# A mixture-of-experts kernel on one core: x loaded first, quaternions as rows, the bias of z written by ScalarE, five low halves subtracted by GpSimd

## What is computed

```python
# x: (8, 512, 256), so 4096 tokens of 256; 8 experts with a hidden width of 1024, the best 2 per token
def cond(x):                       # gate over the sequence, then a quaternion rotation
    x_filtered = ifft(fft(x_quat, axis=1) * spectral_gate, axis=1).real
    return hamilton(q_left_n, hamilton(x_filtered, q_right_conj))
def ffn(x):
    h = x @ W_in + b_in                                  # z in the kernel
    logits = h @ W_gate + b_gate
    topv, topi = top_k(softmax(logits), 2)
    topv = topv / sum(topv)
    mid  = relu(einsum('nd,edh->neh', h, W1) + b1)
    eout = einsum('neh,ehd->ned', mid, W2) + b2
    return (sum over the two choices of topv * eout) @ W_out + b_out
out = x + ffn(cond(x))
```

## Time and profile before

| | |
|---|---|
| median of 3 runs | 512.32 us (510.97 to 513.12) |
| profiled execution | 515.1 us, its span 513.2 us |
| TensorE busy | 494.9 us, 96% of the span |
| VectorE busy | 380.6 us, 74% |
| ScalarE busy | 283.2 us, 55% |
| GpSimd busy | 217.5 us, 42% |
| granted TensorE clock | 1.000 |
| DMA | 80.62 MB |

### The profile page before, as it was taken

The page is one execution under the profiler, slowest core; times in us unless marked ns, Lnnn a source line. Parts: engine busy times, 40 slices in busy tenths (PEclk is TensorE's granted clock), DMA queues, the critical chain, the costliest instruction groups (busy, mean ns, idle before and its releaser), DMA issues.

```text
span 513.2 us, 14538 instructions
## 1 busy us (share of the span) xinstructions
PE 494.9 (96%) x4658; PEld 430.7 (84%) x4659; DVE 380.6 (74%) x742; ACT 283.2 (55%) x576; POOL 217.5 (42%) x264
## 2 busy tenths in 40 slices
PE   7889998899999999999999999999899999999997
PEld 7556687788888888888888888889799999998786
DVE  4789987677786776878768787676568887864675
ACT  3533544655666556665566665336668778780221
POOL 4500025048456384464844637435545453321121
PEclk9999999999999999999999999999999999999999
DMA  6406534846556464555645543433354445133983
GB/s 225 158 2 209 190 125 124 237 143 205 139 172 188 140 213 131 164 179 155 198 144 163 175 122 93 115 100 99 91 163 150 135 130 150 34 114 126 406 333 140
DMA packets 75812, 80.62 MB, mean 157 GB/s; under 512 B 42983, under 2 KB 61740, under 8 KB 74732
## 3 DMA queue, kind: packets, MB, share of 16 engines
q1 hardware_dynamic: 56912, 41.44, 26.2%
q0 software_dynamic: 7936, 22.29, 13.0%
q10 hardware_dynamic: 10908, 16.17, 9.9%
HBM read 53.40 MB, written 26.48 MB: 156 GB/s over the span
## 4 chain that ended last, share of the span: by engine, by line
PE 83%; DMA 5%; issue 5%; DVE 3%; ACT 2%; ACTq 1%; SPq 0%; another core or an unknown queue 0%; DVEq 0%
PE bank L1399 24%; PE bank L1386 10%; PE bank L1325 8%; PE bank L1326 7%; PE bank L1327 7%; PE bank L1218 5%; PE bank L1455 5%; PE bank L1372 4%; PE bank L1374 4%; PE bank L1373 4%; DMA gq<-rows_by_slot 2%; DMA w1s<-y_by_choice 1%; PE bank L1465 1%; PE bank L1188 1%; DMA brow<-in_L_ffn_b_in 1%
## 5 line engine op out<-in xcount | busy, mean ns | idle before, releaser
L713 ACT ACTIVATE region<-bank,b1p,cbits 128x256 f32<-128x256 f32 (+1 forms) x368 | 163.1, 522 | 131.9 <-PE bank L1327 51.7
L567 POOL DMA_INDIRECT y_by_choice<-region,dst x71 | 87.3, 1229 | 166.9 <-DVE region L1063 151.5
L1399 PE MATMUL bank<-w2s,region 128*128 x1200 | 136.0, 273 | 0.9 <-issue 0.7
L1399 PEld LDWEIGHTS bank<-w2s,region 128*128 128x128 f16 x1200 | 116.7, 98 | 16.7 <-issue 2.9
L1094 DVE TENSOR_TENSOR region<-region 128x512 f16<-128x512 f32 (+1 forms) x184 | 104.0, 575 | 27.7 <-ACT region L697 20.4
L1325 PE MATMUL bank<-region,w1s 128*128 128x256 f16 x384 | 104.7, 273 | 4.3 <-DVE region L1100 2.2
L1327 PE MATMUL bank<-region,w1s 128*128 128x256 f16 x384 | 104.7, 273 | 0.0
L1326 PE MATMUL bank<-region,w1s 128*128 128x256 f16 x384 | 104.7, 273 | 0.0
L559 POOL DMA_INDIRECT region<-z_by_token,src x71 | 71.9, 1013 | 75.4 <-DVE src L1020 50.6
L1090 DVE CAST region<-region 128x512 f16<-128x512 f32 x100 | 46.0, 460 | 52.1 <-ACT region L713 47.9
L1372 PE MATMUL bank<-region 128*128 128x128 f16 x336 | 57.5, 219 | 1.1 <-DVE region L1100 0.5
(11 more groups left out here) (267 smaller groups left out, 644.4 us busy)
## 6 DMA issues: line engine op xcount, KB each, us to landing
region<-in_L_ffn_W ACTq DMA_DIRECT2D x14, 1024.0 KB
rows_by_slot<-region SPq DMA_DIRECT2D x33, 256.0 KB
gq<-rows_by_slot SPq DMA_DIRECT2D x132, 64.0 KB
w1s<-y_by_choice SPq DMA_DIRECT2D x12, 512.0 KB, 11.1
w1s<-in_x SPq DMA_DIRECT2D x8, 512.0 KB, 8.3
z_by_token<-w1s SPq DMA_DIRECT2D x16, 256.0 KB, 2.1
region<-in_L_ffn_W SPq DMA_DIRECT2D x2, 1024.0 KB
region<-in_x SPq DMA_DIRECT2D x8, 256.0 KB
```

Of the source, the lines that this page charges most:

```text
L567: g.indirect_dma_start(out=ybuf, out_offset=bass.IndirectOffsetOnAxis(ap=at, axis=0), in_=ysb[:, a % 2, h, :], in_offset=None).then_inc(s_ ...
L713: m = s.activation(midf[:, b, c * n:(c + 1) * n], FB[b][:, c * n:(c + 1) * n], ACT.Relu, bias=b1p[:, bass.ds(r, 1), f:f + 1].rearrange("p ...
L1399: last = mm(YB[par][:, h * D:(h + 1) * D], mids[:, par, l, b, c * TS + h * P:c * TS + (h + 1) * P], w2_at(e, w, f), start=(f == 0 and l == ...
```

## The change

- Loads. `load_channels` and `load_gate` are gone. The quaternion, condition and gate values come in as rows (`qrow`), twice each, on the sync queue, and TensorE transposes them into a bank. ScalarE's queue starts with x groups 0 and 1 and `W_in`; the sync queue loads groups 2 to 7. `b3f` becomes `binb`, b_in on all 128 partitions.
- Opening. TensorE's first dummy products go from 18 to 9, and 4, 3 and 5 dummy products are put at later places. `weff` is multiplied once, scaled, and then transposed on TensorE. x pairs use four banks (`XTB`).
- z. Five dummy products overwrite the five banks. `z_bias` on ScalarE writes the bias into a bank ahead of each pair, and the four products add to it. For the pairs 4, 6, 8, 10 and 12 (`ZPOOL`) ScalarE also copies the scaled bank in full into SBUF (`z_full`, in the buffer `gq`), and GpSimd subtracts the high half from that; VectorE does the other eleven.
- Order. x maxima 5, 6 and 7 and the scale of z come later in VectorE's list; `powers` and `expert_exponents` stand behind `src`; `norms` stands behind `rows_of_slots`.

```diff
-            load_channels(sp, 0)
-            sp.dma_start(winr[:], W_in.rearrange("(k p) n -> p k n", p=P)).then_inc(s_win, 16)
-            for g in range(NG):
-                sp.dma_start(xin[:, g * XG:(g + 1) * XG], tokens(x_h, g * XG, XG)).then_inc(s_x[g], 16)
+            for half in range(2):
+                sp.dma_start(qrow[0:4, half, :], q_right).then_inc(s_q, 16)
+                sp.dma_start(qrow[4:4 + NCOND, half, :], cond).then_inc(s_q, 16)
+            load_x(sp, 2)
+            for half in range(2):
+                sp.dma_start(qrow[4 + NCOND:5 + NCOND, half, :], gate).then_inc(s_gt, 16)
+            for g in range(3, NG):
+                load_x(sp, g)
             sp.dma_start(wout[:], W_out.rearrange("(k p) n -> p k n", p=P)).then_inc(s_late, 16)
...
-            pool.wait_ge(s_b3f, 16)
-            for q in range(3):
-                link(g.tensor_copy(b3r[:, q, :], b3f[:, q, :]))
-                if q < 2:
-                    link(g.tensor_tensor(b3f[:, q + 1, :], b3f[:, q, :], b3r[:, q, :], ALU.subtract))
-            link(g.tensor_scalar(bpc[:, 0, :], b3r[:, 0, :], ident[0:3, 0:1], None, ALU.mult))
-            for q in range(1, 3):
-                link(g.tensor_scalar(bpc[:, 1, :], b3r[:, q, :], ident[0:3, q:q + 1], None, ALU.mult))
-                link(g.tensor_tensor(bpc[:, 0, :], bpc[:, 0, :], bpc[:, 1, :], ALU.add))
-            g.tensor_copy(bin3[:, 0:D], bpc[:, 0, :])
-            g.tensor_copy(bin3[:, D:2 * D], bpc[:, 0, :]).then_inc(s_b3, 1)
...
+            for n, i in enumerate(ZPOOL):
+                pool.wait_ge(s_zc, i + 1)
+                pool.wait_ge(s_zf, n + 1)
+                g.tensor_tensor(zst[:, i, :, 1, :], zfull[:, n % 2], zst[:, i, :, 0, :], ALU.subtract
+                                ).then_inc(s_zg, 1)
             pool.wait_ge(s_idx, 1)
             pool.wait_ge(s_zst, 16 * NP)
...
-            load_channels(act, 1)
+            def copy_xt(i):
+                act.wait_ge(s_xtp, i + 1)
+                s.activation(xt_sb[:, i].rearrange("p t k c -> p (t k c)"), XTB[i % 4][:], ACT.Copy
+                             ).then_inc(s_xt, 1)
+
+            load_x(act, 0)
+            load_x(act, 1)
+            act.dma_start(winr[:], W_in.rearrange("(k p) n -> p k n", p=P)).then_inc(s_win, 16)
             act.dma_start(brow[0:E * KF, :], b1.rearrange("e (c p) -> (e c) p", p=P)).then_inc(s_brow, 16)
             act.dma_start(brow[E * KF:E * KF + KD, :], b_in.rearrange("(k p) -> k p", p=P)).then_inc(s_brow, 16)
-            for half in range(2):
-                load_gate(act, half)
+            act.wait_ge(s_id, 1)
+            s.activation(qsq[:, 14:16], ident[:, 0:2], ACT.Sqrt)
+            copy_xt(0)
             act.dma_start(wgr[:], W_gate.rearrange("(k p) n -> p k n", p=P)).then_inc(s_small, 16)
             act.dma_start(bgr[:], b_gate.rearrange("(a e) -> a e", a=1)).then_inc(s_small, 16)
-            act.dma_start(b3f[:, 0, :], b_in.partition_broadcast(3)).then_inc(s_b3f, 16)
+            copy_xt(1)
+            act.dma_start(binb[:, 0, :], b_in.partition_broadcast(P)).then_inc(s_binb, 16)
+            copy_xt(2)
             act.wait_ge(s_n2, 1)
             s.activation(nrm[:, 1, :], nrm[:, 0, :], ACT.Sqrt).then_inc(s_root, 1)
+            copy_xt(3)
             s.activation(nrm[:, 8, :], nrm[:, 0, :], ACT.Exp, scale=0.0)
...
+            def z_full(n):
+                if n >= 2:
+                    act.wait_ge(s_zg, n - 1)
+                s.activation(zfull[:, n % 2], ZB[ZPOOL[n] % NZ][:].rearrange("p (c k) -> p c k", k=KD), ACT.Copy,
+                             scale=sx[:, 0:1].bitcast(f32)).then_inc(s_zf, 1)
...
-            for i in range(NP // 2):
+            for i in range(4, 11):
                 copy_xt(i)
             copy_logits(0)
-            for i in range(NP // 2, NP):
+            for i in range(11, NP):
                 copy_xt(i)
-                if i == 10:
+                if i == 13:
                     exp(0)
-                if i == 9:
+                if i == 12:
                     act.wait_ge(s_we, 1)
                     s.activation(zj[:], weff.rearrange("p k d -> p (k d)"), ACT.Square,
                                  accum_out=bss[:, E + 1:E + 2]).then_inc(s_wsq, 1)
             copy_logits(1)
+
+            def z_bias(i):
+                if i - NZ in ZPOOL:
+                    act.wait_ge(s_zf, ZPOOL.index(i - NZ) + 1)
+                elif i >= NZ:
+                    act.wait_ge(s_zlo, ZDVE.index(i - NZ) + 1)
+                else:
+                    act.wait_ge(s_zcl, i + 1)
+                s.activation(ZB[i % NZ][:].rearrange("p (t d) -> p t d", t=2), binb[:].to_broadcast([P, 2, D]), ACT.Copy
+                             ).then_inc(s_zb, 1)
+
+            act.wait_ge(s_binb, 16)
+            for i in range(2):
+                z_bias(i)
             exp(1)
+            for i in range(2, NZ):
+                z_bias(i)
             act.wait_ge(s_sx, 1)
             act.wait_ge(s_wsq, 1)
             for i in range(NP):
                 z_out(i)
-                if i == 8:
+                if i in ZPOOL:
+                    z_full(ZPOOL.index(i))
+                if 1 <= i <= NP - NZ:
+                    z_bias(i + NZ - 1)
+                if i == 9:
                     w1_squares(0)
-                if i == 10:
+                if i == 11:
                     w2_squares(0)
...
-                if i >= NZ:
-                    pe.wait_ge(s_zlo, i - NZ + 1)
-                if i == NZ - 1:
-                    pe.wait_ge(s_sx, 1)
-                mm(ZB[i % NZ][:], ones3[:], bin3[:], start=True, stop=False, skip_group_check=True)
+                pe.wait_ge(s_zb, i + 1)
...
-            for i in range(2):
+            for i in range(3):
                 x_pair(i)
+            pe.wait_ge(s_gt, 16 * 2)
+            tr(bank[6][:, 0:1 + NQ], qrow[:].rearrange("q h c -> q (h c)"), ident[0:NQ + 1, 0:NQ + 1]
+               ).then_inc(s_gp, 1)
+            pe.wait_ge(s_brow, 16 * 2)
+            tr(bank[7][:, 0:NR], brow[:], ident[0:NR, 0:NR]).then_inc(s_btp, 1)
+            pe.wait_ge(s_const, 1)
+            spin(bank[5], 4)
             pe.wait_ge(s_rt, 1)
             pe.wait_ge(s_win, 16)
             for ki in range(KD):
                 for kj in range(KD):
-                    mm(bank[1][:, ki * D:(ki + 1) * D], rt[:, kj, ki * P:(ki + 1) * P], winr[:, kj, :],
-                       start=(kj == 0), stop=(kj == KD - 1))
-            for kd in range(KD):
-                for kj in range(KD):
-                    last = mm(bank[6][:, kd * D:(kd + 1) * D], winr[:, kj, kd * P:(kd + 1) * P], rt[:, kj, :],
+                    last = mm(bank[1][:, ki * D:(ki + 1) * D], rt[:, kj, ki * P:(ki + 1) * P], winr[:, kj, :],
                               start=(kj == 0), stop=(kj == KD - 1))
             last.then_inc(s_wep, 1)
-            for i in range(2, 5):
+            for i in range(3, 7):
                 x_pair(i)
             pe.wait_ge(s_we, 1)
+            for ki in range(KD):
+                for kd in range(KD):
+                    last = tr(bank[6][:, kd * D + ki * P:kd * D + (ki + 1) * P], weff[:, ki, kd * P:(kd + 1) * P],
+                              ident[:])
+            last.then_inc(s_wtp, 1)
+            for i in range(7, 9):
+                x_pair(i)
+            pe.wait_ge(s_wt, 1)
             pe.wait_ge(s_small, 16 * 2)
             pe.wait_ge(s_const, 1)
...
             pe.wait_ge(s_wg, 1)
+            spin(bank[5], 3)
             logits_half(0)
-            x_pair(8)
+            x_pair(11)
             logits_t(0)
-            for i in range(9, NP):
+            for i in range(12, NP):
                 x_pair(i)
+            spin(bank[5], 5)
             logits_half(1)
-            pe.wait_ge(s_xmx, NG + 1)
-            tr(bank[5][0:1, 0:P], xmax[:, NG + 1:NG + 2], ident[:]).then_inc(s_xm1, 1)
+            pe.wait_ge(s_ml, 1)
+            for i in range(NZ):
+                mm(ZB[i][:], ones16[:], iota16[:].rearrange("p c q -> p (c q)").unsqueeze(1).to_broadcast([P, 2, 2 * P]),
+                   start=True, stop=True).then_inc(s_zcl, 1)
             logits_t(1)
-            pe.wait_ge(s_b3, 1)
             z_pair(0)
-            pe.wait_ge(s_xm2, 1)
-            pe.wait_ge(s_bsq, 1)
-            pe.wait_ge(s_wsq, 1)
-            mm(bank[5][:, 256:256 + E + 2], ones[:], bss[:], start=True, stop=True)
-            mm(bank[5][:, 192:193], ones[0:1, :], xtop[:], start=True, stop=True).then_inc(s_xm3, 1)
             z_pair(1)
             pe.wait_ge(s_m, LG)
             m_et = m16[:].rearrange("p e t -> p (e t)")
             mm(TB[0][:, 0:E * NT], before[:], m_et, start=True, stop=True)
             mm(TB[0][:, E * NT:2 * E * NT], ones16[:], m_et, start=True, stop=True).then_inc(s_rank, 1)
-            for i in range(2, NP):
+            z_pair(2)
+            pe.wait_ge(s_xmx, NG + 1)
+            tr(bank[7][0:1, 0:P], xmax[:, NG + 1:NG + 2], ident[:]).then_inc(s_xm1, 1)
```

(18 more changed lines are left out.)

## The result

| | before | changed |
|---|---|---|
| median of 18 runs each | 512.2 us | 515.58 us (512.75 to 518.37) |
| profiled execution, its span | 515.1, 513.2 us | 516.36, 514.6 us |
| second choices end | 36.30 | 33.24 |
| slot map ends (T) | 72.67 | 73.28 |
| first gather starts | 72.97 | 75.08 |

The ratio is 1.0075, with a 95% interval of 1.0054 to 1.0097. On 512.2 that is 3.8 us; the medians lie 3.4 apart. The forecast was 515.0. The number was close, but its terms were not: they missed in both directions and happened to cancel. What follows is mostly about that.

What follows compares the result with a forecast made beforehand. TensorE and VectorE were taken as nearly level up to the slot map's end, which moves the rest. Terms -2.4 + 0.1 + 5.1 + 0.2 = +3.0, rounded down to +2.7 on 512.32, gave 515.0 us; range 509.2 to 517.8.

Steps and rivals of the forecast that it cites:

- Opening, -2.4: Start to second choices: row loads and four x banks end the second choices at 33.9 instead of 36.30, 2.4 us earlier.
- Rival C, late rows: Opening: rows queue behind x and land at 8.1, so it gains 0.3, not 2.4; with hold-up 517.1 us; chance 0.13.
- VectorE from there to T without hold-ups, +0.1: Second choices to slot map's end: work taken off VectorE is offset by moved-in maxima and waits; 36.5 against 36.4 us.
- The waits for banks: VectorE during z: new waits because ScalarE frees banks for their bias in order; 2.5 us with handovers.
- the opening's gain is eaten by what moved behind it: VectorE behind the second choices: two x maxima with their reduction, formerly between the two halves, add 2.65 us there.
- Hold-up, +5.1: VectorE during z: GpSimd's five subtractions, 1.24 us each, block it while both read SBUF; 5.1 us later, ends 0 and 7.2.
- Rival B, no hold-up: During z: GpSimd's reads slip between VectorE's or fall on low halves and waits; about 510.2 us; chance 0.32.
- Sum up to T, +2.8 (75.5): Start to slot map's end: opening, VectorE's list and hold-up together move that end 2.8 us later, to 75.5.
- Behind T, +0.2: After the slot map: z's last store leaves 2.0 us before T, takes 2.1 to land, delays the gather 0.2 us.
- TensorE's clock, no term: Whole kernel: the sum gave no time to a lower TensorE clock; the opening's cold start was to cost nothing.
- half speed in z's gaps: TensorE during z: products at half speed in the gaps were listed as a sign of a wrong forecast; no size given.
- The first gather at 75.8: Behind the slot map: expected start of GpSimd's first gather in the forecast case; 70.7 without hold-up.

Runs made afterwards that it cites:

- e7: e5 with the maxima of the last two x blocks moved into the gaps where VectorE waits for logits; ratio 1.0006 to the kernel before.
- e11: e10 plus the x maxima of e7, the maximum's transpose ahead of z pair 0, z's scale right behind the second choices; ratio 0.9958 to the kernel before.
- e4: e1 with five dummy two-operand subtractions on GpSimd, on words nobody uses; ratio 1.0062 to the kernel before.
- e8: e4 with GpSimd's dummy subtractions replaced by one-operand multiplications by a constant; ratio 1.0011 to the kernel before.
- e9: Changed kernel with low half 13 ahead of VectorE's last one-hot product and W2's squares behind the last z output; ratio 1.0038 to the kernel before.
- e10: e5 with W2's squares behind the last z output and low halves 12 and 13 ahead of VectorE's last one-hot product; ratio 0.9988 to the kernel before.
- e2: Changed kernel with 24 dummy products on TensorE ahead of the second half of the slot rows; ratio 1.0041 to the kernel before.
- e12: e11 with 16 dummy products on TensorE ahead of its wait for the third tile's rows; ratio 1.0010 to the kernel before.
- e1: Changed kernel with all sixteen low halves on VectorE, without ScalarE's full copies and GpSimd's subtractions; ratio 1.0020 to the kernel before.
- e5: e1 with 70 dummy products in place of 52 between the slot rows and the first gathered rows; ratio 1.0010 to the kernel before.
- e3: Kernel before with only ScalarE's full copies of five z pairs and their subtraction on GpSimd added; ratio 0.9997 to the kernel before.
- e6: Changed kernel with the first expert's powers and exponents back between low halves 13 and 14, norms behind z pair 13; ratio 1.0084 to the kernel before.

## Why the prediction was right, and where it was not

The direction came from the right mechanism: VectorE and GpSimd hold each other up, and that eats more than the opening gains. The closeness of the number is luck.

- *Opening, -2.4: measured -3.1.* Quaternions read at 6.68 (forecast 6.4), scaled W at 13.37 (13.45), first logits 18.36 (18.7), second 25.05 (25.7). Mechanism right, size 0.7 short. Rival C, late rows, is out.
- *VectorE from there to T without hold-ups, +0.1: measured -0.55* (40.04 less 4.22 is 35.82, against 36.37). The waits for banks were 0.25, 0.61 and 1.27, 2.1 in all for the 2.5 forecast. That the opening's gain is eaten by what moved behind it, 2.3 us of maxima, held; e7 and e11 show that it can be had back only with TensorE's part moved along.
- *Hold-up, +5.1: measured 4.2*, and e4 shows the mechanism and why it is less: what falls on low halves is free. Rival B, no hold-up, is out. "SBUF — State Buffer" of the Trainium skill, section "Who interferes with whom", says that a two-input VectorE instruction and a GpSimd one that reads SBUF block each other fully. The rows with a two-input GpSimd instruction agree (1.26 for 0.42); those with a one-input one, in e8, do not (1.33 for 1.33 beside it, 0.60 for 0.17), and the measurement decides. One undisturbed subtraction took 1.15 in e4, where I had 1.24.
- *Sum up to T, +2.8 (75.5): measured +0.6 (73.3).* Three terms erred in one direction.
- *Behind T, +0.2: measured +1.5* on the gather. This step failed: the last store was to leave 2.0 before T and to land in 2.1. It left 1.4 before T, since the issue of the one ahead of it took 1.13, and landed 3.4 behind its low half. e9 and e10 show that the order of the stores is not why.
- *TensorE's clock, no term: about 1.7 us* (estimate from e2). The prediction named half speed in z's gaps only as a sign that it would be wrong. In the changed kernel's profile the clock stayed up in z; it fell where the sum did not look, ahead of the second slot rows and of the third tile. In e4, e11 and e12 it did fall in z's gaps.

So 515.0 against 515.6 came from a map forecast 2.2 us too late and two costs behind it, 1.3 and 1.7 us, that were missing. The verdict of slower rests on the hold-up (without it, e1, no difference is measured), the store and the clock. The parts of the change were not taken apart further: no run has the new opening or ScalarE's bias alone. The first gather at 75.8 was forecast for the wrong reason too: it started at 75.08, released by the store.

## What to carry to other kernels

Work given to GpSimd while VectorE is full of steps that read SBUF is not free: price it by what VectorE loses, and place it beside instructions with an operand in PSUM. The price depends on what it meets: five subtractions cost 4.2, 2.4 and 1.7 us in three kernels here. When an engine gets work earlier, move what hangs on it in the other engines' lists as well, or the gain becomes waits. And when TensorE is relieved, ask where it will now stand idle: idle times of 2.1 to 4.0 us were often, not always, followed by the lower clock here. Dummy products in one such gap took the ratio from 1.0075 to 1.0041 (e2), in another they changed nothing that can be measured (e5), and in a third they made the kernel slower (e12).

## What the runs showed of the hardware

- A GpSimd multiplication by a constant, 128x512 float32 to float16, took 1.50 to 1.52, longer than the subtraction of two operands of that size, 1.15.
- A GpSimd instruction that finds VectorE in a long two-operand step waits for its end (2.15 and 2.19 for 1.5 and 1.1) and goes ahead of VectorE's next.
- The clock fell behind idle times of, among others, 2.14 (e3), 2.17 (e11), 2.34 (e1), 2.93 and 3.41 (changed kernel) and 4.04 us (e6). It stayed behind 2.17 (e1, e5, e7 and e10), 2.19 (before), 2.46 (e8) and 3.07 (e9). So the idle time alone does not tell; what else does is open.
- Equal stores of 256 KB on one queue, issued in 0.32 us each, landed in 2.5, 3.4, 2.0 and 2.0 us: the last four of the kernel before, in order.
